# Graph attention with a windowed scatter: messages as the stationary operand in every group, and SiLU in pieces of 512 columns

## The reference, cut to what matters

```
w   = silu(edge_feats @ rad_W1 + rad_b1) @ rad_W2 + rad_b2
w  += silu(chi_scalar @ sph_W1 + sph_b1) @ sph_W2 + sph_b2          # [edges, 128]
q, k, v = x @ Wq, x @ Wk, x @ Wv
alpha = (q[receivers] * w * k[senders]) summed over each of 8 heads of 16, / 4, * cutoffs
out   = segment_sum(alpha * v[senders], receivers) / 16             # [6250, 128]
x     = layernorm(x + out)
```

## Time and profile before

| | |
|---|---|
| median of 3 executions | 2755.45 us (2751.88 to 2758.18) |
| the profiled execution | 2762.11 us, its span 2760.2 us |
| mean granted PE clock over the span | 0.77 of full speed |
| busy time: PE / PEld / DVE / ACT / POOL | 1905.8 / 1496.6 / 1581.1 / 712.5 / 1537.5 us |
| POOL's first and last gather by L701 | 56.2 and 2690.7 us |

### The profile page before, as it was taken

How to read it: one execution, slowest core, us unless ns; L and a number is a source line. 1 busy time by engine, 2 the same in 40 slices (tenths; PEclk the granted TensorE clock), 3 DMA queues, 4 the chain that set the end, 5 groups by cost and what they waited for, 6 DMA issues and landing times.

```text
span 2760.2 us, 40664 instructions
## 1 busy us (share of the span) xinstructions
PE 1905.8 (69%) x14110; PEld 1496.6 (54%) x14110; DVE 1581.1 (57%) x4221; ACT 712.5 (26%) x1030; POOL 1537.5 (56%) x1626
## 2 busy tenths in 40 slices
PE   6457666666677666766667677777677777777777
PEld 5345545555455455555555555555555555555555
DVE  3256555555555555555565565565565555655558
ACT  3222222222222222222222222222222222222224
POOL 5545555555555555555556555556555565555561
PEclk8677887778777787777777877777777777777778
DMA  7534443434344434434344444344344344344441
GB/s 247 172 117 126 119 126 113 126 111 129 113 127 114 125 116 122 128 113 129 111 127 132 120 129 133 117 131 133 116 132 133 115 133 133 114 134 131 121 130 48
DMA packets 166897, 348.12 MB, mean 126 GB/s; under 512 B 60797, under 2 KB 71912, under 8 KB 166696
## 3 DMA queue, kind: packets, MB, share of 16 engines
q0 software_dynamic: 76928, 209.56, 26.7%
q1 hardware_dynamic: 88358, 132.90, 14.7%
q10 hardware_dynamic: 1410, 3.07, 0.4%
HBM read 330.44 MB, written 14.95 MB: 125 GB/s over the span
## 4 chain that ended last, share of the span: by engine, by line
PE 36%; another core or an unknown queue 23%; DVE 20%; issue 19%; DVEq 1%; ACT 1%; DMA 0%; ACTq 0%; SPq 0%
PE bank L739 20%; DVE t L1049 5%; PE bank L782 4%; PE bank L757 4%; PE hidden L716 3%; PE bank L729 3%; DVE oh L940 2%; DVE ot L934 2%; DVE msg L1069 2%; DVE part L964 2%; DVE accT L990 2%; DVE t L1036 1%; PE hidden L325 1%; PE bank L465 1%
## 5 line engine op out<-in xcount | busy, mean ns | idle before, releaser
L701 POOL DMA_INDIRECT kvt<-kvtab,srcS x1584 | 1501.1, 948 | 1151.0 <-DVE msg L1069 688.1
L828 ACT ACTIVATE hs<-hidden,B 128x1024 f32<-128x1024 f32 x404 | 427.2, 1108 | 1639.2 <-remote 997.4
L739 PE MATMUL bank<-W2r,hs 128*128 128x128 f32 x3224 | 631.8, 357 | 25.2 <-ACT hs L828 17.5
L739 PEld LDWEIGHTS bank<-W2r,hs 128*128 128x128 f32 x3224 | 543.7, 255 | 128.6 <-issue 98.2
L739 PE MATMUL bank<-W2s,hs 128*128 128x128 f32 x3224 | 570.7, 335 | 5.9 <-issue 5.6
L739 PEld LDWEIGHTS bank<-W2s,hs 128*128 128x128 f32 x3224 | 541.6, 253 | 5.4 <-issue 5.1
L1036 DVE TENSOR_TENSOR t<-bank,kvt 128x512 f32<-128x512 f32 x395 | 271.8, 688 | 435.5 <-remote 249.6
L757 PE MATMUL bank<-msg,oh 128*32 128x128 f32 x3200 | 209.7, 341 | 413.5 <-issue 251.6
L757 PEld LDWEIGHTS bank<-msg,oh 128*32 128x32 f32 x3200 | 76.2, 121 | 623.4 <-issue 518.9
L1049 DVE TENSOR_TENSOR t<-bank,t 128x512 f32<-128x512 f32 x402 | 275.9, 686 | 238.0 <-remote 227.7
L782 PE MATMUL bank<-cS,part 128*128 128x32 f32 x704 | 152.1, 303 | 308.7 <-DVE part L964 303.8
(11 more groups left out here) (130 smaller groups left out, 680.2 us busy)
## 6 DMA issues: line engine op xcount, KB each, us to landing
dbt<-dst SPq DMA_DIRECT2D x102, 512.0 KB, 5.6
eft<-in_ef SPq DMA_DIRECT2D x102, 512.0 KB, 6.9
kvt<-kvtab,srcS POOLq DMA_INDIRECT x1584
qwt<-qtab SPq DMA_DIRECT2D x202, 32.0 KB
kvtab<-kvt SPq DMA_DIRECT2D x24, 256.0 KB, 2.0
qtab<-qx SPq DMA_DIRECT2D x12, 384.0 KB
out<-partn SPq DMA_DIRECT2D x48, 64.0 KB
accT<-in_xT SPq DMA_DIRECT2D x5, 512.0 KB
```

The source lines that it names most:

```text
L701: pool.indirect_dma_start(kvt[:, (g - HX) % KS, t, :], None, kvtab, bass.IndirectOffsetOnAxis(ap=srcS[:, g * TG + t:g * TG + t + 1], axis= ...
L739: m = pe.matmul(WB[g % 2][:, t * D:(t + 1) * D], hs[:, g % HS, j, t * 128:(t + 1) * 128], w2[:, :], start=(g < 2 and j == 0 and t == 0), s ...
L828: act.activation(hs[:, 2 * p % HS:2 * p % HS + n, j, :], hidden[:, 0:2 * n, :].rearrange("p (a j) f -> p a j f", j=2)[:, :, j, :], ACT.Sil ...
```

## The change

The scatter of every group is done as that of the last one was: messages stationary, the one-hot streamed, the four tiles accumulated in PSUM as 128 features x 32 nodes. `part`, `fold`, `fold_tiles`, the semaphore `m_fold` and the collects of strips go. A collect is left only for the 48 groups with a layer-norm block, and copies that block alone (128 x 128). `accumulate` waits for `m_sc` in place of `m_fold` and does the scaling (`scalar_tensor_tensor` with 1/64). `silu` is called for each group, with one ACTIVATE over 512 columns a net that waits for its own `l1` matmul; `l1` and `l2` wait for the matching counts of `m_si`.

```diff
-                if g < NE and g % 2 == 0:
-                    silu(g // 2)
+                if g < NE:
+                    silu(g)
...
                 for t in range(TG):
-                    m = pe.matmul(strips(g)[32 * t:32 * t + W, 0:D], oh[:, g % WS, t, :], msg[:, g % MS, t, :],
-                                  start=True, stop=True)
+                    m = pe.matmul(sums(g), msg[:, g % MS, t, :], oh[:, g % WS, t, :],
+                                  start=(t == 0), stop=(t == TG - 1))
...
-            def fold_tiles(g):
-                pe.wait_ge(m_part, g + 1)
-                pe.matmul(strips(g)[:, 2 * D:2 * D + W], parts(g), fold,
-                          start=True, stop=True).then_inc(m_fold, 1)
...
                     if p >= 1:
-                        pe.wait_ge(m_si, 2 * (p - 1) + i % 2 + 1)
+                        pe.wait_ge(m_si, 4 * (p - 1) + i + 1)
...
             def l2(g):
-                pe.wait_ge(m_si, 2 * (g // 2) + 2)
+                pe.wait_ge(m_si, 2 * g + 2)
...
                 for j in range(2):
-                    act.activation(hs[:, 2 * p % HS:2 * p % HS + n, j, :],
-                                   hidden[:, 0:2 * n, :].rearrange("p (a j) f -> p a j f", j=2)[:, :, j, :],
-                                   ACT.Silu, bias=B1[:, j:j + 1]).then_inc(m_si, 1)
+                    i = 2 * g + j
+                    act.wait_ge(m_l1, i + 1)
+                    act.activation(hs[:, g % HS, j, :], HB[i % 4][:, :], ACT.Silu,
+                                   bias=B1[:, j:j + 1]).then_inc(m_si, 1)
...
-                if 0 <= g - 2 < LC:
+                if g - 2 in use_n and g - 2 < LC:
                     collect(g - 2)
...
-                dve.wait_ge(m_fold, g + 1)
                 if g >= 1:
                     dve.wait_ge(m_acc, g)
-                dve.tensor_tensor(accT[:, bass.ds(at, W)], accT[:, bass.ds(at, W)], strips(g)[:, 2 * D:2 * D + W],
-                                  ALU.add).then_inc(m_acc, 1)
...
+                dve.wait_ge(m_sc, g + 1)
...
                 dve.scalar_tensor_tensor(accT[:, bass.ds(at, W)], strips(g)[:, 2 * D:2 * D + W], 1.0 / 64,
                                          accT[:, bass.ds(at, W)], ALU.mult, ALU.add).then_inc(m_acc, 1)
```

More of the change, by code:

```diff
@@ L141, in gnn_program @@
         sp, pool, act, dve, pe = nc.sync, nc.gpsimd, nc.scalar, nc.vector, nc.tensor
-        hidden = ctx.enter_context(nc.psum_tensor("hidden", [128, 4, 512], f32))
-        HB = [hidden[:, i, :] for i in range(4)]
-        bank = HB + [ctx.enter_context(nc.psum_tensor(f"bank{i}", [128, 512], f32)) for i in range(4, 8)]
+        bank = [ctx.enter_context(nc.psum_tensor(f"bank{i}", [128, 512], f32)) for i in range(8)]
+        HB = bank[0:4]
         WB = bank[4:6]
@@ L157, in gnn_program @@
         npass = sb("npass", [1, 1], i32)
-        cS = sb("cS", [128, 1 + W + 3 + 256 + W], f32)
+        cS = sb("cS", [128, 1 + W + 3 + 256], f32)
         pidx = cS[:, 0:1]
@@ L162, in gnn_program @@
         centre = cS[:, 4 + W:4 + W + 128]
-        fold = cS[:, 4 + W + 256:4 + W + 256 + W]
         eye = cS[:, 4 + W + 128:4 + W + 256]
@@ L593, in gnn_program @@
         oh = sb("oh", [128, WS, TG, W], f32)
-        part = sb("part", [128, 2, D], f32)
-        partn = sb("partn", [128, 2, 2 * D], f32)
+        partn = sb("partn", [128, 2, D], f32)
         hs = sb("hs", [128, HS, 2, G], f32)
@@ L639, in store @@
                 sp.wait_ge(m_y, c + 1)
-                sp.dma_start(out[c * 128:(c + 1) * 128, :], partn[:, c % 2, D:2 * D]).then_inc(m_out[c % 2], 16)
+                sp.dma_start(out[c * 128:(c + 1) * 128, :], partn[:, c % 2, :]).then_inc(m_out[c % 2], 16)
             def rows(b):
@@ L748, in strips, with sums @@
                 return HB[NE - 1 - g] if g >= NE - 3 else SB
+            def sums(g):
+                return strips(g)[:, 2 * D:2 * D + W]
             def scat(g):
@@ L752, in scat @@
                 if g >= NE - 3:
-                    pe.wait_ge(m_si, 2 * NP)
+                    pe.wait_ge(m_si, 2 * NE)
                 elif g >= 1:
@@ L770, in scat_whole @@
                         pe.wait_ge(m_msg, g + 1)
-                    m = pe.matmul(strips(g)[:, 2 * D:2 * D + W], msg[:, g % MS, t, :], oh[:, g % WS, t, :],
+                    m = pe.matmul(sums(g), msg[:, g % MS, t, :], oh[:, g % WS, t, :],
                                   start=(t == 0), stop=(t == TG - 1))
                 m.then_inc(m_sc, 1)
[L775 to L778, removed]
-            def fold_tiles(g):
-                pe.wait_ge(m_part, g + 1)
-                pe.matmul(strips(g)[:, 2 * D:2 * D + W], parts(g), fold,
-                          start=True, stop=True).then_inc(m_fold, 1)
             l1(0)
@@ L795, in gnn_program @@
                     scat(g - 3)
-                if g >= 3:
-                    fold_tiles(g - 3)
                 if g < NE - 2:
@@ L803, in gnn_program @@
             scat(NE - 2)
-            fold_tiles(NE - 3)
-            fold_tiles(NE - 2)
             scat_whole(NE - 1)
@@ L853, in square @@
             def square(c):
-                g = at_n[c]
-                act.wait_ge(m_part, g + 1)
+                act.wait_ge(m_part, c + 1)
                 if c >= 1:
                     act.wait_ge(m_sq, c)
-                act.activation(sq[:, 0, :], partn[:, c % 2, D:2 * D], ACT.Square, scale=D ** -0.5,
+                act.activation(sq[:, 0, :], partn[:, c % 2, :], ACT.Square, scale=D ** -0.5,
                                accum_out=ss[:, c:c + 1]).then_inc(m_sq, 1)
@@ L865, in scale_by @@
             def scale_by(c):
-                act.activation(partn[:, c % 2, D:2 * D], partn[:, c % 2, D:2 * D], ACT.Copy,
+                act.activation(partn[:, c % 2, :], partn[:, c % 2, :], ACT.Copy,
                                scale=rs[:, c:c + 1]).then_inc(m_y, 1)
             def late_collect(g):
+                c = use_n[g]
                 act.wait_ge(m_sc, g + 1)
[L871 to L879, removed]
+                if c >= 2:
+                    act.wait_ge(m_out[c % 2], 16 * (c // 2))
+                act.activation(partn[:, c % 2, :], strips(g)[:, D:2 * D], ACT.Copy).then_inc(m_part, 1)
             for g in range(NE + 12):
-                if g < NE and g % 2 == 0:
-                    silu(g // 2)
+                if g < NE:
+                    silu(g)
                 if 2 <= g < NE:
@@ L893, in gnn_program @@
                     act.dma_start(cutS[:, SE:T], cutT[:, SE:T]).then_inc(m_cut, 16)
-                if LC <= g - 4 < NE - 1:
+                if g - 4 in use_n and g - 4 >= LC:
                     late_collect(g - 4)
@@ L954, in collect @@
             def collect(g):
+                c = use_n[g]
                 dve.wait_ge(m_sc, g + 1)
[L956 to L964, removed]
+                if c >= 2:
+                    dve.wait_ge(m_out[c % 2], 16 * (c // 2))
+                dve.tensor_copy(partn[:, c % 2, :], strips(g)[:, D:2 * D]).then_inc(m_part, 1)
             def first_guess(c):
@@ L986, in accumulate @@
                 at = dve.snap(dve_base[g % 4], min_val=0, max_val=NQ - W)
-                dve.wait_ge(m_fold, g + 1)
                 if g >= 1:
                     dve.wait_ge(m_acc, g)
-                dve.tensor_tensor(accT[:, bass.ds(at, W)], accT[:, bass.ds(at, W)], strips(g)[:, 2 * D:2 * D + W],
-                                  ALU.add).then_inc(m_acc, 1)
[L993 to L997, removed]
                 dve.wait_ge(m_sc, g + 1)
+                if g in use_n and g >= LC:
+                    dve.wait_ge(m_part, use_n[g] + 1)
                 dve.scalar_tensor_tensor(accT[:, bass.ds(at, W)], strips(g)[:, 2 * D:2 * D + W], 1.0 / 64,
@@ L1106, in gnn_program @@
                 dve.reciprocal(rs[:, c:c + 1], var[:, c:c + 1]).then_inc(m_rr, 1)
-            accumulate_whole(NE - 1)
+            accumulate(NE - 1)
             dve.wait_ge(m_acc, NE)
@@ L1157, in feat @@
         return a.reshape(ng, G, R).transpose(0, 2, 1)
-    cst = np.zeros((128, 1 + W + 3 + 256 + W), np.float32)
+    cst = np.zeros((128, 1 + W + 3 + 256), np.float32)
     cst[:, 0] = np.arange(128) // NPART
@@ L1164 @@
     cst[:, 4 + W + 128:4 + W + 256] = np.eye(128)
-    cst[:, 4 + W + 256:] = np.tile(np.eye(W), (128 // W, 1)) / 64.0
     w1 = np.concatenate([arr(L0_gnn_rad_W1), arr(L0_gnn_sph_W1)] * 2, 0)
```

12 lines of the change are left out of this document (5 added, 7 removed).

## The result

The changed kernel takes 2931.78 us (median of 4 runs, 2913.03 to 2954.0), the kernel before 2753.66 (4 runs, 2750.28 to 2758.18): 1.0636 times as long, 95% interval 1.0578 to 1.0693. The prediction was 2648 us, so the sign was wrong, and the time lies above the range. The kernel before was run again beside each set of experiments, and the median of its fast runs (there is also a slower state) went from 2714 to 2755 us from set to set, so that runs of different sets are compared by their ratios.

A forecast was written before the change was run, and what follows sets the result against it. POOL was taken to bound the kernel, with its gathers and 688 us of pauses. Terms of -90, -59 and +40 summed to -109 us from 2762, 2653 profiled, stated as 2648 us; range 2520 to 2880.

The forecast's parts named there:

- What bounds the kernel: POOL's gathers and its 198 pauses for a message; the change can save almost only in the pauses' 688 us.
- the second term: Gather runs ended by DVE's collect: t2 decides instead, half gaining and half losing, -59 us (bounds -284 and +39).
- the half that was to gain 1.6 us a pause: Collect-ended runs where t2 comes slightly later, POOL stops and results clear: 49 x 1.6 us gained.
- The first term: Gather runs ended by t2: collect and fold leave the way to the message, -90 us (bounds -20 and -160).
- The 100 pauses: POOL pauses put to t2, out of 198, each to shrink by 0.9 us; the other 98 put to collect.
- The third: Scatter on PE gets dearer by 0.47 to 0.78 us a group, partly covered: +40 us (bounds 0 and +154).
- The nothings: Single SiLUs on ACT, accumulate's wait for the scatter, l1's waits and the kernel's end: put at nothing.
- The end: Last 11 groups, bound by DVE: DVE loses 0.2 us each, PE gains that much work, 0 to -5 us.
- the fold's 309: PE's idle time before fold matmuls, 309 us, by which PE's idle time was to fall.
- Rival A: Gather runs all grow to three groups and end at t1, 127 pauses of 5.8 us: 2850 us, chance 0.26.
- Rival C: PE becomes the bound, all 0.47 to 0.78 us on the path of 400 groups: about 2950 us, chance 0.06.
- a rule of the Trainium skill: PE's scatter with 32 streamed columns would cost four times the old; at most +228 us in place of +154.

The follow-up runs named there:

- e7: Kernel before with gathers for only the first 15 groups of the ring, later groups reusing those rows: 1717.08 us, ratio 0.6208.
- e8: Changed kernel with gathers for only the first 15 groups of the ring, later groups reusing those rows: 1828.65 us, ratio 0.6612.
- e4: Changed kernel with DVE waiting, ahead of cutoff and message, for the scatter of two groups back, copying nothing: 2711.07 us, ratio 0.9838.
- e3: Changed kernel with the short scatter again (one-hot stationary, message streamed into four strips, strips not added up): 2937.76 us, ratio 1.066.
- e6: Changed kernel with DVE's message held for the scatter two groups back and the short four-strip scatter, strips not added up: 2698.81 us, ratio 0.9768.
- e5: Changed kernel, nothing held, with PE doing the second layer of g ahead of the scatter of g-3: 2797.11 us, ratio 1.031.
- e12: Changed kernel with POOL's gather into the buffer of group m also waiting for the scatter of m-1: 2604.85 us, ratio 0.9551.
- f1: Kernel before with POOL's gather into the buffer of group m also waiting for the scatter of m-1: 2616.03 us, ratio 0.965.

## Why the prediction was wrong

**What bounds the kernel** was right: POOL's gathers with their pauses, and the pauses are ended by late results. e7 shows what gathers and pauses cost together, 1717 us without them. In e7 and e8 late results are all but gone: DVE's t1 and t2 have three waits of the "remote" kind in the two runs together, 24.8 us.

**The step that failed** is the second term, -59 us, "in runs that collect ends, t2 decides instead". It saw that a run may grow and stop at t1, and priced that pause rightly: 5.8 us, measured 5.87. What it had wrong is how often such a stop comes and for how few groups. It let one come only after three groups without a pause, charged 0.4 us for two groups, and so had 49 x 0.4 = 20 us of loss. The trace has 75 such stops, and they cost 193 us: 31 after runs of three, at 1.66 us a run, but 30 after runs of one, at 3.9 us a run, each just behind a pause of under 2 us. As the row after 0.83 us shows, such a pause did not make the next result come in time. And the half that was to gain 1.6 us a pause, 78 us in all, is not there: all other runs together gain 35 us, with what the first term gives. The wait in the removed collect was counted as a cost to be shed; e4 shows it was worth more than the copy and fold were.

**The first term, -90,** had its direction right and its condition wrong. e4 keeps the wait and sheds copy and fold: its ratio of 0.9838 is 45 us of 2754, the dearer scatter included. Where nothing holds the message or the gather, no run shows the gain. The 100 pauses were too many as well: by DVE's longest wait, 64 of 193 pauses before end with t2 and 122 with a collect (L964, L962).

**The third, +40,** can't be told from none beside gathers (e3, e6). Eight scatter matmuls were put at 1.4 to 1.7 us; the timeline has them at 1.05 and 1.89, and the group's mean is 524.7/402 = 1.31.

**The nothings** held but for the end: the pieces alone 1.0009, the SiLU 687 ns, and accumulate idles 2.2 us in all. The end, put at 0 to -5 us, came out 8 longer: in the two profiles it is 69.5 us from the last gather's start before and 77.6 after. PE's idle time did not fall by the fold's 309: before scatters alone it went from 413 to 835 us.

**The rivals.** Rival A named the place (t1, longer runs, slower) and the size of the pause, and gave 2850, range 2800 to 2930; the median lies just above. But not every run grew to three groups: of its 127 pauses of nearly 6 us the trace has 75, and only 31 are behind runs of three. Rival C's time, 2950, is near by accident: its mechanism needs the scatter's price, and e3 takes that away without gain. The prediction set a rule of the Trainium skill beside C (TensorEngine Tiling (Array Packing), Performance Considerations: with a short streamed dimension, swap the operands and tile the columns). Without gathers the trace goes its way, in size far below the 1.15 us a group drawn from it: e8 is slower than e7 by 0.28 (112/403), net of the copies and folds. Beside gathers e3 shows nothing of it.

**Still open:** why results that PE owes come so late while gathers run. The runs show that they do, and that it ends soon after the last gather, not by what means. Nor is it shown why 30 of 31 runs of three are followed by a run of one, or why e5's exchange takes half the loss away when a shorter scatter takes none.

## What to carry to other kernels

A wait that seems only to delay may pace another engine: before removing it, ask which engine stops because of it, and what is left to do on the chain when that stop ends. If the others' results come late while one engine issues transfers, try holding the transfers so that the computing engines run ahead: the wait on POOL made the kernel before 3.5% faster with one line. And test a dear operation by its price and by its order in separate kernels, since here a lower price alone gained nothing and the order decided.

## What the hardware showed that was not expected

The same eight scatter matmuls of the changed kernel took 1.05 us inside a run and 1.89 us at a restart, where PE had waited 5.29 us. The windows of those two stretches grant the full clock (2.4 GHz) and half of it (1.2 GHz):

```profile
845.60:846.70 1.10, 1.07 (x9) 1.10 (x10) 1.03 (x5) 0.42 (x1) 0.80 (x2) 1.00 0.30 63
863.20:865.20 2.00, 1.89 (x9) 1.92 (x10) 1.93 (x6) 0.45 (x1) 0.00 (x0) 0.50 0.11 25
```

It is not this one case: before 75 of the 403 scatters of the trace PE had stood for over 5 us, and all of these took 1.74 to 1.89 us. So such a pause is followed by a slow stretch of PE, on the way to the next t1. And a gather does not always take the same time: 948 ns in the kernel before, 962 in the changed kernel, 975 in e12 and 1002 in f1. The last two are 27 and 54 ns more on 1584 gathers, which is 43 and 86 us of POOL's time. The length of the pauses does not order these figures, as the changed kernel pauses most. Why was not tried.

```profile
L699 POOL DMA_INDIRECT kvt<-kvtab,srcS x1584 | 1544.9, 975 | 953.0 <-issue 431.8
```

```profile
L702 POOL DMA_INDIRECT kvt<-kvtab,srcS x1584 | 1586.9, 1002 | 926.5 <-issue 459.7
```
